# A decoder layer on one core: normalisation to ScalarE, stores to SyncE, first heads' maxima spread, token side of the feed-forward a tile ahead

## The reference

```python
x = x + attn(layernorm(x), Wq, Wk, Wv, Wo)          # ctx @ Wo.T at its end
x = x + xattn(layernorm(x), ctx, ctx)
x = x + ffn(layernorm(x), w_gate, w_up, w_down)

def _layernorm(x):       return (x - mean(x)) / sqrt(var(x) + 1e-5)
def xattn(q, k, v):      # q, k, v: (4*8, 64, 512); 32 heads of 64 rows
    sm = softmax(einsum('bdm,bdn->bmn', q, k) * 64 ** -0.5)
    return einsum('bmn,bcn->bcm', sm, v)
def _quant_act(x):       s = max(abs(x), -1) / 127 + 1e-5; return clip(round(x / s), -128, 127), s
def ffn(x, ...):         # qlinear: both sides quantised, I = 2048
    return qlinear(silu(qlinear(x, w_gate)) * qlinear(x, w_up), w_down)
```

## Time and profile before

| | us |
|---|---|
| median of 3 runs | 835.95 |
| the profiled execution | 833.68, its span 831.5 |
| PE / DVE / ACT / POOL busy | 762.8 / 657.7 / 469.0 / 416.3 |
| mean granted TensorE clock | 0.982 of full |
| granted clock in 660:680, 680:700, 700:720 us | 1.00, 0.91, 1.00 |
| output projection, 381.25 to 449.20: PE / DVE / ACT busy | 55.92 / 49.49 / 19.94 of 67.95 |
| GpSimd's instructions on 128x1, veps and rstd, mean | 0.34 and 0.57 |
| xh on ScalarE and xl on VectorE, mean | 0.63 and 0.66 |
| the two stores of a tile on ScalarE's queue | 0.33 and 0.45 |
| sums and products of a pair of heads at 638.8, on the chain | 1.06 and 3.43 |

### The profile page before, as it was taken

The page is one execution under the profiler, slowest core; times in us unless marked ns, Lnnn a source line. Parts: engine busy times, 40 slices in busy tenths (PEclk is TensorE's granted clock), DMA queues, the critical chain, the costliest instruction groups (busy, mean ns, idle before and its releaser), DMA issues.

```text
span 831.5 us, 14270 instructions
## 1 busy us (share of the span) xinstructions
PE 762.8 (92%) x4258; PEld 405.4 (49%) x4306; DVE 657.7 (79%) x1937; ACT 469.0 (56%) x828; POOL 416.3 (50%) x421
## 2 busy tenths in 40 slices
PE   5999989999999999997886899999997998999996
PEld 4877544444444444445664555445443443444442
DVE  7676878889898898844778877888885787899983
ACT  4566556766676676773222666666664454344451
POOL 5544489999992000002221577788777343433321
PEclk9999999999999999999998899999998999999999
DMA  8898754454432122102565556655541233444544
GB/s 295 303 348 284 204 180 128 146 159 129 138 104 70 50 61 63 50 2 79 193 230 200 148 147 172 169 164 162 167 129 48 51 61 74 102 90 89 90 94 96
DMA packets 112028, 113.61 MB, mean 137 GB/s; under 512 B 70640, under 2 KB 82160, under 8 KB 108880
## 3 DMA queue, kind: packets, MB, share of 16 engines
q1 hardware_dynamic: 104992, 91.27, 39.7%
q0 software_dynamic: 1840, 12.98, 4.6%
q10 hardware_dynamic: 5120, 8.46, 2.8%
HBM read 81.26 MB, written 20.51 MB: 122 GB/s over the span
## 4 chain that ended last, share of the span: by engine, by line
PE 24%; DVE 12%; issue 6%; POOL 5%; DMA 3%; SPq 2%; ACT 2%; DVEq 0%; ACTq 0%; POOLq 0%
PE r_p L1499 7%; PE r_pn L1456 4%; DVE r_mx L1279 2%; PE r_pn L1515 2%; PE r_p L1419 2%; PE r_p L1444 2%; PE r_p L1445 2%; PE r_pd L1515 2%; DVE r_stats L1245 2%; DMA r_rden<-inverse_sums 2%; PE r_pd L1466 2%; POOL r_h L1126 1%; DVE r_lo L1253 1%; DVE r_h L1318 1%; DVE tok L1259 1%
## 5 line engine op out<-in xcount | busy, mean ns | idle before, releaser
L778 ACT ACTIVATE b_probs<-ab_j 128x512 f32<-128x512 f32 (+1 forms) x352 | 176.7, 560 | 30.7 <-PE ab_j L843 14.0
L147 DVE CUSTOM_DVE_ANT_0 b_junk<-ab_t,mask_qk 128x128 bf16<-128x128 f32 (+2 forms) x243 | 108.8, 485 | 27.2 <-PE ab_t L127 26.9
L843 PE MATMUL ab_j<-qs,ks 98*128 98x512 bf16 (+1 forms) x352 | 122.6, 363 | 2.4 <-DMA qs<-mrow 1.2
L1169 ACT ACTIVATE r_probs<-r_p 128x512 f32<-128x512 f32 x128 | 74.4, 593 | 64.9 <-PE r_p L1445 63.7
L147 DVE CUSTOM_DVE_ANT_0 b_junk<-ab_e,mask_qk 128x256 bf16<-128x256 f32 (+2 forms) x237 | 104.1, 482 | 4.5 <-PE ab_e L127 4.2
L1279 DVE TENSOR_REDUCE r_mx<-r_p 128x1 f32<-128x512 f32 x128 | 84.9, 685 | 14.1 <-PE r_p L1419 13.0
L1100 POOL TENSOR_TENSOR r_halves<-r_probs 128x1024 f32<-128x1024 f32 x32 | 76.5, 2389 | 24.7 <-ACT r_probs L1169 22.5
L861 PE MATMUL ab_pv<-b_probs,v 128*32 128x512 f32 (+3 forms) x1024 | 75.5, 436 | 0.0
L127 PE MATMUL ab_e<-ks,qs 96*128 96x128 bf16 (+3 forms) x269 | 64.4, 302 | 9.7 <-DMA ks<-k_parts 4.5
L1219 ACT ACTIVATE r_silu<-r_p,r_cg 128x512 f32<-128x512 f32 x64 | 42.3, 679 | 54.6 <-PE r_p L1499 52.7
L1499 PE MATMUL r_p<-wu,r_zt 128*128 128x512 bf16 x251 | 66.0, 384 | 5.5 <-DVE r_h L1318 5.3
(11 more groups left out here) (162 smaller groups left out, 1662.0 us busy)
## 6 DMA issues: line engine op xcount, KB each, us to landing
r_k<-in_ctx SPq DMA_DIRECT2D x64, 128.0 KB, 2.7
r_qh<-x_normed_high SPq DMA_DIRECT2D x64, 128.0 KB, 2.8
qs<-q_parts SPq DMA_DIRECT2D x32, 192.0 KB, 3.3
q_parts<-a_parts SPq DMA_DIRECT2D x15, 384.0 KB, 6.9
a_wst<-in_w_gate SPq DMA_DIRECT2D x4, 1024.0 KB, 8.5
a_wst<-in_w_up SPq DMA_DIRECT2D x4, 1024.0 KB, 10.6
a_wst<-in_w_down SPq DMA_DIRECT2D x4, 1024.0 KB, 9.1
qs<-q_parts SPq DMA_DIRECT2D x32, 128.0 KB, 2.8
```

Of the source, the lines that this page charges most:

```text
L147: best = nc.vector.tensor_tensor_reduce(out=junk[:, 2 * (st.use[i, k] % slots) + n, 0:w], in0=bank[:, c:c + w], in1=keep["mask_qk"][:, SEQ ...
L778: nc.scalar.activation(pblock(j % 2, kb)[:, j0:j0 + nj, c:c + w], p2[(NE * j + n) % BANKS2][:, 0:nj * w].rearrange("p (j c) -> p j c", j=n ...
L843: last = nc.tensor.matmul(bank, ks[0:STACK + 2, s, kb * P:(kb + 1) * P], qs[0:STACK + 2, s, j0:j0 + nj, kb * P + c:kb * P + c + w], start= ...
L1169: nc.scalar.activation(probs[:, j % PSLOTS, n, :], p2[(KD * j + n) % BANKS][:], ACT.Exp, scale=SCALE).then_inc(exps, 1)
```

## The change

Output projection: VectorE's `xn` becomes an activation of ScalarE (scale rstd, bias -mean times rstd), for which GpSimd makes the bias `shift` with a third 128x1 instruction. VectorE's `xl` moves from step j+2 to j+3 and ahead of `tok`. The stores go from ScalarE's queue to SyncE's program, ahead of which SyncE waits for xl. Attention steps 0 to 2 disappear as such: their loads, key splittings and first scores with their maxima are laid over steps 4 to 15 of the output projection (`early`), one maximum a step from step 8 on. Steps 3 and 4 stand behind steps 17 and 18.

Feed-forward: from step 2 on the token side of tile i is done in step i, between the third and the fourth product; the moments and the result move ahead of the second product. `cg` and `cu` get a third buffer. SyncE runs every feed step one attention step later (`behind=1`). PE's down(12) is held until behind gate and up of tile 15, and its result to the end of that step.

```diff
--- before.py
+++ after.py
...
         C_LAST, D_LAST, E_LAST = TILES + 3, HEADS_X + 11, TILES + 5
-        D_EARLY = 4
+        HELD, LATE = TILES - 4, 2
+        D_FIRST, D_BESIDE = 3, 2
         E_BESIDE = {HEADS_X - 1: 0, HEADS_X + 1: 1}
         E_BESIDE.update({HEADS_X + 3 + k: 2 + k for k in range(D_LAST - HEADS_X - 3)})
 
-        def in_turn(attend_output, attend_context, feed):
-
-            for i in range(C_LAST):
-                attend_output(i)
-                if i >= C_LAST - D_EARLY:
-                    attend_context(i - (C_LAST - D_EARLY))
-            for i in range(D_EARLY, D_LAST):
+        def in_turn(attend_output, early, attend_context, feed, behind=0):
+
+            for c in range(C_LAST):
+                attend_output(c)
+                early(c)
+                if c >= C_LAST - D_BESIDE:
+                    attend_context(D_FIRST + c - (C_LAST - D_BESIDE))
+            for i in range(D_FIRST + D_BESIDE, D_LAST):
                 attend_context(i)
-                if i in E_BESIDE:
-                    feed(E_BESIDE[i])
-            for i in range(len(E_BESIDE), E_LAST):
+                if i - behind in E_BESIDE:
+                    feed(E_BESIDE[i - behind])
+            for i in range(len(E_BESIDE) - behind, E_LAST):
                 feed(i)
 
+        KEYS_AT = {6: 0, 8: 1, 12: 2}
+
+        def score_at(c):
+
+            return (1 + (c - 8) // KD, (c - 8) % KD) if 8 <= c < 16 else None
+
         TURN = 1
 
...
         @block.sync
...
+                j = i - 3
+                if 0 <= j < TILES:
+                    sp.wait_ge(C["xl"], j + 1)
+                    for name, tile in (("xh", xh), ("xl", xl)):
+                        sp.dma_start(scr[name][P * j:P * (j + 1), :], tile[:, j % UNROLL, :].bitcast(F32)).then_inc(stored[j % UNROLL], 16)
+
+            def early(c):
+                if c == 4:
+                    load_context_rows(0)
+                    load_context_rows(1)
+                elif c == 5:
+                    load_query_rows(0)
+                    load_query_rows(1)
+                elif c == 7:
+                    load_query_low(0)
+                    sp.wait_ge(kl_done, 1)
+                    load_context_rows(2)
+                elif c == 9:
+                    load_query_rows(2)
+                    load_query_rows(3)
+                    load_query_low(1)
+                elif c == 11:
+                    sp.wait_ge(qh_in[0], 32)
+                    load_query_rows(4)
...
+                if i >= LATE:
+                    turn_tokens(i)
-            in_turn(attend_output, attend_context, feed)
+            in_turn(attend_output, early, attend_context, feed, behind=1)
...
         @block.gpsimd
...
+                j = i - 1
+                if 0 <= j < TILES:
+                    s = j % 2
+                    c = slice(s, s + 1)
+                    pool.wait_ge(C["aggr"], j + 1)
+                    pool.sem_inc(keep["pool_passed"], 1)
+                    nc.gpsimd.tensor_scalar(veps[:, c], mv[:, s, 1:2], LN_EPS, None, ALU.add).then_inc(C["veps"], 1)
+                    pool.wait_ge(C["veps"], 2 * j + 1)
+                    if due(j - 1):
+                        pool.wait_ge(C["normed"], j - 1)
+                    nc.gpsimd.tensor_tensor(rstd[:, c], veps[:, c], keep["minus_half"][:, 0:1], ALU.pow).then_inc(C["veps"], 1)
+                    pool.wait_ge(C["veps"], 2 * j + 2)
+                    nc.gpsimd.tensor_scalar(shift[:, c], mv[:, s, 0:1], rstd[:, c], -1.0, ALU.mult, ALU.mult).then_inc(C["rstd"], 1)
...
+                if i <= LATE:
+                    round_tokens(i - 1)
                 if i < TILES:
                     deviation(S, i)
+                if i >= LATE:
+                    round_tokens(i)
...
         @block.scalar
...
                 j = i - 2
                 if 0 <= j < TILES:
+                    act.wait_ge(C["rstd"], j + 1)
+                    if due(j - 1):
+                        act.wait_ge(C["xl"], j - 1)
+                    nc.scalar.activation(xn[:, j % 2, :], tok[:, j, :], ACT.Identity, bias=shift[:, j % 2:j % 2 + 1],
+                                         scale=rstd[:, j % 2:j % 2 + 1]).then_inc(C["normed"], 1)
                     act.wait_ge(C["normed"], j + 1)
                     if due(32 * (j // UNROLL)):
                         act.wait_ge(stored[j % UNROLL], 32 * (j // UNROLL))
                     nc.scalar.activation(xh[:, j % UNROLL, :], xn[:, j % 2, :], ACT.Copy).then_inc(C["xh"], 1)
-                j = i - 3
-                if 0 <= j < TILES:
-                    act.wait_ge(C["xl"], j + 1)
-                    for name, tile in (("xh", xh), ("xl", xl)):
-                        act.dma_start(scr[name][P * j:P * (j + 1), :], tile[:, j % UNROLL, :].bitcast(F32)).then_inc(stored[j % UNROLL], 16)
+
+            def early(c):
+                if c in KEYS_AT:
+                    keys(KEYS_AT[c])
+                    if KEYS_AT[c] == 2:
+                        keys_high(0)
...
+                            act.wait_ge(C["projected"], TILES)
+                        elif j == 1:
+                            act.wait_ge(C["x1"], TILES)
+                        elif j == 2:
                             act.wait_ge(C["xl"], TILES)
-                        elif j == 1:
-                            act.wait_ge(C["projected"], TILES)
-                        elif j == 2:
-                            act.wait_ge(C["x1"], TILES)
...
+                def quantised(j):
+                    if not 0 <= j < TILES:
+                        return
+                    act.wait_ge(S["xr"], j + 1)
+                    if due(16 * (j // 2)):
+                        act.wait_ge(zt_in[j % 2], 16 * (j // 2))
+                    nc.scalar.activation(zq[:, j % 2, :], zn[:, j % 2, :], ACT.Copy, bias=-MAGIC).then_inc(S["xq"], 1)
                 gate(0)
...
                         nc.scalar.activation(hq[:, j % 2, half], h[:, j % 2, half], ACT.Copy, bias=-MAGIC).then_inc(S["hq"], 1)
                 gate(1)
-                j = i - 1
-                if 0 <= j < TILES:
-                    act.wait_ge(S["xr"], j + 1)
-                    if due(16 * (j // 2)):
-                        act.wait_ge(zt_in[j % 2], 16 * (j // 2))
-                    nc.scalar.activation(zq[:, j % 2, :], zn[:, j % 2, :], ACT.Copy, bias=-MAGIC).then_inc(S["xq"], 1)
+                if i <= LATE:
+                    quantised(i - 1)
                 gate(2)
                 gate(3)
-
-            in_turn(attend_output, attend_context, feed)
+                if i >= LATE:
+                    quantised(i)
...
         @block.vector
...
                     dve.wait_ge(C["hi"], i + 1)
                     nc.vector.tensor_tensor(lo[:, i % 2, :, :], tr[i % 2], hi[:, i % 2, :, :].bitcast(F32),
                                             ALU.subtract).then_inc(C["lo"], 1)
+                j = i - 3
+                if 0 <= j < TILES:
+                    dve.wait_ge(C["xh"], j + 1)
+                    nc.vector.tensor_tensor(xl[:, j % UNROLL, :], xn[:, j % 2, :], xh[:, j % UNROLL, :].bitcast(F32),
+                                            ALU.subtract).then_inc(C["xl"], 1)
                 j = i - 1
                 if 0 <= j < TILES:
                     dve.wait_ge(C["projected"], j + 1)
                     dve.wait_ge(x_in[j % UNROLL], 16 * (j // UNROLL + 1))
                     nc.vector.tensor_tensor(tok[:, j, :], pj[j % 2][:], o_in[:, j % UNROLL, :], ALU.add).then_inc(C["x1"], 1)
                     dve.wait_ge(C["x1"], j + 1)
+                    if due(j - 1):
+                        dve.wait_ge(C["rstd"], j - 1)
                     moments(C, j, tok[:, j, :])
-                j = i - 2
-                if 0 <= j < TILES:
-                    dve.wait_ge(C["xh"], j + 1)
-                    nc.vector.tensor_tensor(xl[:, j % UNROLL, :], xn[:, j % 2, :], xh[:, j % UNROLL, :].bitcast(F32),
-                                            ALU.subtract).then_inc(C["xl"], 1)
-                j = i - 1
-                if 0 <= j < TILES:
-                    dve.wait_ge(C["rstd"], j + 1)
-                    nc.vector.tensor_scalar(xn[:, j % 2, :], tok[:, j, :], mv[:, j % 2, 0:1], rstd[:, j % 2:j % 2 + 1],
-                                            ALU.subtract, ALU.mult).then_inc(C["normed"], 1)
-
...
+            def early(c):
+                if score_at(c) is not None:
+                    i, n = score_at(c)
+                    maximum(i, n)
+                    if n == TURN - 1:
+                        keep_maxima(i)
+                if c in KEYS_AT:
+                    keys_low(KEYS_AT[c])
...
+                if i <= LATE:
+                    scale_tokens(i - 1)
                 product(0)
                 chunk_max(0)
-                j = i - 5
-                if 0 <= j < TILES:
-                    dve.wait_ge(S["down"], j + 1)
-                    dve.wait_ge(S["cd"], j + 1)
```

(21 more changed lines are left out.)

188 lines of the change are left out of this document (106 added, 82 removed).

## The result

The changed kernel took 828.75 us (median of six, 825.76 to 834.42), the kernel before 835.63 in the same rounds (833.36 to 839.08). The ratio is 0.9928, 95% interval 0.9900 to 0.9956: about 6 us faster, 6.9 by the medians. The forecast was 824.7 us with a range of 810 to 831.5, so the time lies inside the range, 4 us above the number.

A forecast was written before the change was run, and what follows sets the result against it. It took the projection as bound by VectorE waiting for GpSimd's rstd, and the feed-forward by a ring nearly PE's 10.36 us. Gains of 7 + 3.4 + 0.8 = 11.2 us off 835.95 gave 824.7 us, range 810 to 831.5.

The forecast's parts named there:

- Output projection: From first to last projection tok: 54.1 us instead of 62.2, 8 us earlier (4 to 10), VectorE's wait for rstd gone.
- The stores' move: Output projection's stores issued by SyncE instead of ScalarE: claimed to gain nothing by itself.
- First heads: Start of cross-attention: head 0 12.8 us earlier, then 10 us to head 1 behind tile 15's stores; head 1 7 earlier.
- the heads keep their pace: Cross-attention behind head 1: the heads run as before, so the whole attention moves by 7 us.
- Attention to feed-forward: Change of stage, clock of before: gate_up(0) at 637.6 instead of 643.48 us, first fh 3.6 us earlier.
- the sum 162.9 us from the first fh to the last: Feed-forward: 143.4 + 18.5 + 1 = 162.9 us against 162.7 before, so the gain of 3.6 us stays 3.4.
- Those waits go: Feed-forward: VectorE's waits for the later rden loads vanish, since the loads come a step ahead of their use.
- The ring: Feed-forward, fh to fh through GpSimd, ScalarE and VectorE: 4.32 + 6.71 = 11.03 us a step in 13 steps, from 10.42.
- The end: Last down products: PE idles 2.9 instead of 3.88 us and down(15) costs 3.6 to 5.3; 0.8 us gained.
- A: Rival, feed-forward: the ring doesn't close, PE keeps 10.36 us a step; 25.8 us gained, 810.2 us; chance 18%.
- B: Rival, output projection: it gains nothing, SyncE bounds it at 4.1 us a tile; 830.8 us; chance 12%.
- C: Rival, feed-forward: PE's 0.67 us wait in every step lowers its clock, costing 24 us; 848.7 us; chance 4%.

The follow-up runs named there:

- vector_norm: not_ahead with the output projection's normalisation on VectorE again, in the order of before; 820.5 us, ratio 0.9804 to the kernel before.
- stores_back: not_ahead with the two stores of a projection tile issued by ScalarE again, as before; 809.6 us, ratio 0.9672 to the kernel before.
- late3: Changed kernel with the token side a tile ahead from feed-forward step 3 instead of step 2; 824.0 us, ratio 0.9852 to the kernel before.
- same_turn: not_ahead with SyncE's feed-forward part in the same turn as the other engines', as before; 822.0 us, ratio 0.9838 to the kernel before.
- ahead_in_cover: stores_back with the token side a tile ahead from step 3, its scaling between the result and the second product; 817.6 us, ratio 0.9785 to the kernel before.
- not_ahead: Changed kernel with the token side never a tile ahead (tile i-1 in step i, as before); 812.8 us, ratio 0.9696 to the kernel before.
- maxima_first: not_ahead with SyncE's transfers of the maxima of heads 0 and 1 ahead of the stores of tiles 14 and 15; 804.7 us, ratio 0.9643.
- no_held: stores_back without the held down product, tile 12's down in its ordinary turn; 810.7 us, ratio 0.9734 to the kernel before.

## Why the number was 4 us off, step by step

- **Output projection: right, 7.5 us for 8.** Two durations were taken too short: GpSimd's shift has a mean of 0.61 us (I took 0.35) and ScalarE's xn 0.82 (0.63). The ring through GpSimd and ScalarE was thus 3.44 us in the middle instead of 3.3, hardly above the 3.5 that VectorE's work gave. vector_norm shows that the normalisation on VectorE, its 0.55 us and the 0.77 of waiting ahead of it together, was the cause; what each makes by itself no run shows.
- **The stores' move: no gain, as forecast, and a loss on top.** stores_back has gate_up(0) 4.0 us earlier, by SyncE's order and not by ScalarE's time.
- **First heads: the mechanism right, the size 9.4 for 7 us.** Both waits stand behind the stores as forecast, but head 0 to head 1 took 8.35 us instead of 10. The terms of that 10 add up to 10.6. Behind it "the heads keep their pace" was wrong: 7.2 us of the 9.4 were left at the last pairs. That this is the 7 of the forecast is luck, two errors that cancel.
- **Attention to feed-forward: gate_up(0) 13.0 us earlier for 12.9, by that luck, first fh 1.4 us late.** The meeting itself gave 5.7 us for 5.9, which is right. Beside GpSimd's additions y took 0.93 and zn 1.49 us.
- **The step that failed: the sum 162.9 us from the first fh to the last, which held no wait of TensorE at the second turn of the overlap.** I followed what zq stood in front of for one exponential, and not for the copy of y in the second turn. First to second fh took 15.05 us instead of 11.03, and the last fh came 167.1 us behind the first. late3 shows it: without the wait the last fh is 4.8 us earlier. "Those waits go" held for rden: its waits did go, all but the first of 6.4 us; same_turn shows SyncE's turn to be the reason.
- **The ring: right to a hundredth**, 11.03 or 11.04 us in nine of the thirteen steps, 11.42 in three, and the long one. That it closes at the scaling's place is shown by ahead_in_cover, whose steps are 10.40; not_ahead, which takes away the tile ahead as well, has 9.89. What I missed is its other side: my sum gave the whole feed-forward +0.2 us and took that for neutral, while the same diff held 16 us (medians of not_ahead and the changed kernel; 19 by the ratios) that its own token side took back.
- **The end: 0.07 us for 0.8.** Within the bounds: down(15) stayed at 5.30.
- **The rivals.** A (TensorE keeps 10.36) didn't come in this kernel, and is what not_ahead does, at 812.8 us against the 810.2 worked out for it. B is out by the 3.44 us a tile, C by the granted clock, 1.00 from 660 to 800 us.
- **Sums.** By their own terms the 3.8 us of the projection's ring are 3.7, the 6.4 from the last tok to head 0 are 6.3 (6.17 measured), and A's 18.8 are 18.9. Nothing hangs on these.

The profiled pair gives 4.9 us and the medians 6.9; executions of this kernel lie up to 9 us apart, so that difference isn't explained further.

## What to carry to other kernels

Work moved one tile ahead isn't free for not being new. Here 1.8 us of scaling a tile cost 11 us over a stage (late3 against not_ahead): 3 by its place between two links of the ring that sets the step, the rest because a tile scaled right behind its own moments stands for GpSimd's answer. The same diff's moments, put into the wait, gave 5.5. Read for each moved operation which side of the step's last wait it lands on, and how far behind it its own input is made. When an operation gets a new place in an in-order list, follow everything behind it for the whole overlap of two stages (SyncE's stores before the maxima: 4 us and more; zq before the copy of y: 4 to 5), not only the first instruction. A change made of parts that sum to little should be split: here the projection's -8, SyncE's turn with -9, the moments' -5.5, the wait for y with +4.7 and the tile ahead with +11 us (medians) hid one another.

## What the runs showed of the hardware

- A subtraction on VectorE with two sources in SBUF takes 0.69 us, and 2.88 when GpSimd's addition over SBUF has begun 0.03 us before it; it then ends 0.54 us behind GpSimd's. Begun 0.26 us ahead of GpSimd's, it takes 0.69. The reductions of VectorE that start during GpSimd's addition in maxima_first keep 0.67 to 0.68. By the Trainium skill, page "SBUF — State Buffer", section "Who interferes with whom", a VectorE instruction with two inputs in SBUF contends with a GpSimd instruction that reads SBUF, and the order of issue decides which of them is blocked; the trace agrees, with 2.88 us in the one order and 0.69 in the other.
- The last down product took 5.30 us behind gaps of 2.56, 2.88 and 3.88 us (changed kernel, no_held, before; granted clock 0.68 over it in all three, part of it at 1.2 GHz), and 3.61 in late3, where the gap was 1.13 us (granted clock 1.00, 2.4 GHz).
- The first tok of the projection came 5.8 us behind the last self-attention tok in some executions and 7.4 to 8.3 in others, with the code the same: the granted clock in these 8.5 us was 1.00 in the changed kernel's profile and 0.80 in not_ahead's. That is why stages are counted from that tok.
- ScalarE's normalisation, with scale and bias from a 128x1 tile each, took 0.816 us a tile where its plain copy of the same 128x512 took 0.633.
